# A graph network on one core: one-hot rows laid out two by two with 16-bit operands in the first stage, and gathered rows awaited by pairs of chunks in the first attention

## What is computed

```python
x = _layernorm(x + _L0_gnn_ref(x, src, dst, ...), axis=-1)   # attention, 8 heads
x = _layernorm(x + _L1_gnn_ref(x, ..., src, dst), axis=-1)   # attention, 4 heads
x = _layernorm(x + _L2_gnn_ref(x, src, dst, ...), axis=-1)   # 5 GIN layers
x = _layernorm(x + _L3_gnn_ref(x, edge_index, ...), axis=-1) # 3 SAGE layers
```

```python
Q = (text_emb @ Wq.T + bq).reshape(N, H, DK)
K = (text_emb @ Wk.T + bk).reshape(N, H, DK)
V = (x @ Wv.T + bv).reshape(N, H, DK)
Q_, K_, V_ = Q[col], K[row], V[row]
scores = jnp.sum(Q_ * (K_ + rel), axis=-1) / np.sqrt(DK)
e = jnp.exp(scores - segment_max(scores, col)[col])
attn = e / segment_sum(e, col)[col]
out = segment_sum(attn[:, :, None] * V_, col).reshape(N, OUT_DIM)
```

## Time and profile before

| | |
|---|---|
| median of 3 runs | 3004.7 us (3004.44 to 3008.03) |
| profiled execution | 3004.63 us, span 3002.9 us |
| mean granted clock of TensorE | 0.941 |
| busy share of the span | PE 88%, DVE 53%, ACT 38%, POOL 33% |
| `prepare` | from the start to about 146 us |
| attention of layer 0 | from about 148 us to about 696 us |

### The profile page before, as it was taken

The page is one execution under the profiler, slowest core; times in us unless marked ns, Lnnn a source line. Parts: engine busy times, 40 slices in busy tenths (PEclk is TensorE's granted clock), DMA queues, the critical chain, the costliest instruction groups (busy, mean ns, idle before and its releaser), DMA issues. The chain is left out here.

```text
span 3002.9 us, 53203 instructions
## 1 busy us (share of the span) xinstructions
PE 2653.7 (88%) x17164; PEld 1925.8 (64%) x17164; DVE 1592.7 (53%) x2777; ACT 1129.3 (38%) x3145; POOL 981.8 (33%) x1020
## 2 busy tenths in 40 slices
PE   6879999998537788877499999999999989999998
PEld 4769999996437777775265555655556556565654
DVE  9589999995568888886421512315123152121123
ACT  6135555554336777764310503105031052121111
POOL 4377777763367777773200100101001000000000
PEclk7889999999869999998599999999999999999999
DMA  6699999982337898884254252442524233444332
GB/s 229 228 312 319 316 317 317 316 295 85 104 85 148 152 162 148 152 161 74 87 182 134 63 152 75 135 131 60 152 74 135 74 109 95 115 119 134 114 112 92
DMA packets 332504, 470.20 MB, mean 157 GB/s; under 512 B 155942, under 2 KB 243062, under 8 KB 331588
## 3 DMA queue, kind: packets, MB, share of 16 engines
q1 hardware_dynamic: 269364, 286.33, 35.9%
q0 software_dynamic: 59088, 176.67, 19.0%
q10 hardware_dynamic: 3776, 3.80, 0.4%
HBM read 412.95 MB, written 55.50 MB: 156 GB/s over the span
## 5 line engine op out<-in xcount | busy, mean ns | idle before, releaser
L1144 ACT ACTIVATE sums<-e_part_ps 128x384 f32 x832 | 413.0, 496 | 382.8 <-PE e_part_ps L1042 291.7
L2464 PE MATMUL gin_sum_ps<-slab,high 128*128 128x391 f16 x2000 | 495.4, 331 | 2.0 <-DMA slab<-adj 1.6
L2464 PE MATMUL gin_sum_ps<-slab,low 128*128 128x391 f16 x1920 | 478.2, 331 | 0.0
L849 POOL DMA_INDIRECT e_from_src<-vk,src x416 | 393.3, 945 | 141.9 <-issue 95.4
L849 POOL DMA_INDIRECT e_from_src<-val,src x416 | 393.3, 946 | 134.0 <-issue 109.4
L2866 PE MATMUL sage_sum_ps<-slab,high 128*128 128x391 f16 x1200 | 389.5, 329 | 0.6 <-DVE x L3007 0.6
L2866 PE MATMUL sage_sum_ps<-slab,low 128*128 128x391 f16 x1152 | 379.3, 329 | 0.0
L2649 DVE SCALAR_TENSOR_TENSOR z_t<-h_t,gin_own,gin_sum_ps 128x391 f32<-128x391 f32 x80 | 44.8, 617 | 481.4 <-PE gin_sum_ps L2464 481.4
L1040 PE MATMUL e_part_ps<-e_onehot,e_from_src 128*128 128x129 f32 x1664 | 284.9, 296 | 13.8 <-ACT ends L1146 11.1
L2526 POOL TENSOR_SCALAR h_t<-h_t 128x391 f32<-128x391 f32 x32 | 40.1, 1263 | 770.5 <-DVE h_t L2679 770.5
L2464 PEld LDWEIGHTS gin_sum_ps<-slab,high 128*128 128x128 f16 x2000 | 195.2, 98 | 130.6 <-DVE low L2641 3.7
(11 more groups left out here) (402 smaller groups left out, 4354.1 us busy)
## 6 DMA issues: line engine op xcount, KB each, us to landing
slab<-adj SPq DMA_DIRECT2D x128, 977.5 KB, 4.8
e_window<-q_part SPq DMA_DIRECT2D x416, 128.0 KB
slab<-adj SPq DMA_DIRECT2D x32, 488.8 KB, 5.0
slab<-adj SPq DMA_DIRECT2D x32, 391.0 KB, 6.3
adj<-e_counts SPq DMA_DIRECT2D x8, 1250.0 KB
adj<-e_counts SPq DMA_DIRECT2D x8, 1193.8 KB
e_from_src<-vk,src POOLq DMA_INDIRECT x416
e_from_src<-val,src POOLq DMA_INDIRECT x416
```

The lines of the kernel that those rows point to most:

```text
L849: nc.gpsimd.indirect_dma_start(from_src[:, b, j, :], None, by_src, bass.IndirectOffsetOnAxis(ap=keep["src"][:, g * G + j:g * G + j + 1], a ...
L1144: nc.scalar.activation(keep["sums"][:, :, bass.ds(starts[j], P)], of[:, :, 0:P], ACT.Copy).then_inc(whole_copied, 1)
L2464: mm = nc.tensor.matmul(sum_ps[KH * n + m][:, 0:AN], part[:, t, m * P:(m + 1) * P], slab[:, s, n, k * AN:(k + 1) * AN], start=(t == 0 and ...
```

## The change

In `prepare` DVE makes all 16 one-hots of a round, ACT none. `is_row` gets the layout `[P, NB, 8, P, 2]`: two chunks lie side by side, row number by row number, so that the innermost pair of elements belongs to two chunks. The numbers 0 to 127 are written twice each (`row_numbers`, `[P, P, 2]`, float16, cast by POOL), and the operand `row_of` is now read as pairs of neighbouring elements, each pair 128 times. Every operand of the instruction is 16-bit with an innermost step of 1. PE reads its weights with a step of two elements. ACT's `spot_side`, its buffers, its two semaphores and the conversion `minus_row` (L378) go; `take_cells` and `take_turned` stand alone in ACT's program. In layer 0's attention each pair of chunks has its own semaphore (16 in place of 4), and each `match` waits for the two gathers of its pair.

```diff
-        iota16 = sb("iota16", [P, P], F16)
-        is_row = sb("is_row", [P, NB, STEP, P], F16)
+        row_numbers = sb("row_numbers", [P, P, 2], F16)
+        is_row = sb("is_row", [P, NB, STEP // 2, P, 2], F16)
...
-            nc.vector.tensor_scalar(minus_row[:, :], ints[:, 2, :], -1.0, None, ALU.mult).then_inc(row_set, 1)
...
-                nc.vector.tensor_tensor(is_row[:, u % NB, SIDE:STEP, :], iota16[:, :].unsqueeze(1).to_broadcast([P, STEP - SIDE, P]),
-                                        row_of[:, u * STEP + SIDE:(u + 1) * STEP].unsqueeze(2).to_broadcast([P, STEP - SIDE, P]),
-                                        ALU.is_equal).then_inc(rows_spotted, 1)
+                nc.vector.tensor_tensor(is_row[:, u % NB, :, :, :], row_numbers[:, :, :].unsqueeze(1).to_broadcast([P, STEP // 2, P, 2]),
+                                        row_of[:, u * STEP:(u + 1) * STEP].rearrange("p (q i) -> p q i", i=2).unsqueeze(2)
+                                        .to_broadcast([P, STEP // 2, P, 2]), ALU.is_equal).then_inc(rows_spotted, 1)
...
-            for u in range(STEPS):
-                spot_side(u)
-                if u in (9, 17, 25):
-                    take_cells(u // BANK - 1)
-                if u in (12, 20):
-                    take_turned(u // BANK - 1)
-            take_turned(2)
-            take_cells(3)
-            take_turned(3)
+            for q in range(4):
+                take_cells(q)
+                take_turned(q)
...
                 pe.wait_ge(rows_spotted, u + 1)
-                pe.wait_ge(side_spotted, u + 1)
...
-                    mm = nc.tensor.matmul(cell_ps[:, FOLD * c:FOLD * (c + 1)], is_row[:, u % NB, j, :],
+                    mm = nc.tensor.matmul(cell_ps[:, FOLD * c:FOLD * (c + 1)], is_row[:, u % NB, j // 2, :, j % 2],
...
-        src_in = sems(nc, ctx, *(f"e{layer}_src_in{b}" for b in range(RING)))
+        LANDED = 1 if layer else PAIRS
+        src_in = [sems(nc, ctx, *(f"e{layer}_src_in{b}_{i}" for i in range(LANDED))) for b in range(RING)]
...
-                        bass.IndirectOffsetOnAxis(ap=keep["src"][:, g * G + j:g * G + j + 1], axis=0)).then_inc(src_in[b], 16)
+                        bass.IndirectOffsetOnAxis(ap=keep["src"][:, g * G + j:g * G + j + 1], axis=0)).then_inc(src_in[b][j * LANDED // G], 16)
...
-                if pair == 0:
-                    v.wait_ge(src_in[b], 16 * G * it + 16 * G)
+                v.wait_ge(src_in[b][pair], 32 * (it + 1))
```

27 lines of the change are left out of this document (5 added, 22 removed).

## The result

The changed kernel takes 2988.12 us (median of 5 runs, 2982.74 to 2995.68). The kernel before, timed again beside it, took 3008.03 us (5 runs, 3004.44 to 3011.67). The ratio is 0.9933, with a 95% interval of 0.9921 to 0.9945, so about 20 us less. The forecast was 2990.7, in a range of 2986 to 2999: the number is 2.6 us off, but as a difference to the kernel before the forecast had 13.9 us and the ratio says 20.1 (16.5 to 23.8). The profiled execution took 2984.15 us, of it 2982.4 us span. The same kernel was measured twice more later on: 0.9949 (0.9929 to 0.9970) and 0.9934 (0.9920 to 0.9949).

A forecast was written before the change was run, and what follows sets the result against it. It took DVE to bound prepare's loop at full clock and PE at half, with PE, DVE and POOL within 1% in the first attention. Loop 10.4 plus attention 3.5, 13.9 us off 3004.6, gave 2990.7 us, range 2986 to 2999.

The forecast's parts named there:

- The spotting, 1.22 us: In prepare's loop, DVE's comparison making 2048 one-hot elements takes 1.22 us, at 0.52 ns an element plus a fixed part.
- The round at full clock, 1.58 us: In prepare's loop, waits through DVE and PE hold 3.15 us for two rounds, 1.58 each: 0.42 us saved a round.
- The round at half clock, nothing saved: In prepare's loop at half clock, PE is the bound and its 2.28 us a round stands, so nothing is saved.
- The loop, 10.4 us: Prepare's loop: 1.8 up to find_edges, 1.1 for two rounds, 7.8 for the last twelve, less 0.3, saves 10.4 us.
- Nothing changes behind the loop: Work from the loop's end to the attention moves earlier whole, with no gain of its own; 1 to 2 us allowed in range.
- The weight step, 0: PE reading placing weights at a step of two in prepare costs 0 to 30 ns a load, taken as 0.
- Rival B: Prepare's weight step costs 30 ns a load, 0.48 us a round, leaving 4.8 us gained: 2999.8 us; chance 0.06.
- ACT's work leaving, 0 by itself: Taking the one-hots from ACT in prepare's loop costs nothing and gives nothing by itself.
- The attention, 3.5 us: In the first attention, waits by pairs leave no wait for match's chunks, and ticks run at 9.94 us: 3.5 us saved.
- A: The faster rate does not come in prepare: spotting 2.28 us, round 2.53, total 3009.8 us, slower than before; chance 0.07.
- C: The clock stays half for long in prepare's loop, giving back 0.70 us a round: 2998.5 us; chance 0.04 wholly, 0.07 in part.
- D: Waits by pairs give nothing in the first attention, since transfers are as full as PE: 2994.2 us; chance 0.06.

The follow-up runs named there:

- e8: The full change with VectorE taking the Q tile of two rounds back instead of one: 2987.65 us, ratio 0.9912 to the kernel before.
- e2: The kernel before with only the attention's waits by pairs added: 3005.32 us, ratio 0.9981 to the kernel before.
- e12: The full change with VectorE taking Q from two rounds back and make_fold ahead of find_edges, no unread matmuls: 2987.50 us, ratio 0.9926.
- e5: The full change, but ScalarE still makes the first 4 of each 16 one-hots, in the new layout: 3001.14 us, ratio 0.9966.
- e4: The full change with the old one-hot layout, VectorE making all 16, waits by pairs kept: 3016.39 us, ratio 1.0026.
- e6: The full change plus 5 unread matmuls, two behind the seventh Q tile and three behind the ninth: 2992.94 us, ratio 0.9919.

## Why the prediction held, step by step

- *The spotting, 1.22 us:* right to the hundredth, 0.52 ns an element and 156 ns fixed against 0.52 and 155. The way to it was weaker than that. The row of 255 ns for 416 elements gives, less the 156 fixed, 0.24 ns an element and not the 0.26 that the prediction reads from it; twice 0.24 would have made 1.13 us. That two sources halve the rate was assumed, and no run tries it. What the runs show is half of the 1.04 ns that the old layout takes. The upper bound (2.28) is real: it is what the old layout takes for the same elements. The Trainium skill ("VectorE: DVE Perf Modes", "The perf-mode tier table") gives 1224 ns for such an operation, and the trace agrees with its 1215.
- *The round at full clock, 1.58 us:* 1.60 over twelve, and the two rows 1.71 and 1.47 show the loop of waits, since it holds two rounds. Taking it away (e8) gave the 1.47 that DVE alone was said to need.
- *The round at half clock, nothing saved:* right where PE is the bound (2.3 us from 31.65 to 33.97), but the four rounds from 9 to 13 took 8.78 us where they took 9.38. Of these 0.6 us 0.53 lie in the first one, right behind `make_fold`, where PE had caught up and DVE was the bound.
- *The loop, 10.4 us:* it was 12.7. Up to the start of `find_edges` 3.1 us against 1.8, and the prediction's most was 1.9: its wait for the gathers (0.49) went wholly, since POOL was done with them 4.9 us earlier (at 34.9 instead of 39.8), and the clock rose at 34 instead of 37 (0.7 us in round 4). From there to spotting 9 0.8 us against 1.1, rounds 9 to 13 0.6 against nothing, the last twelve rounds 7.6 against 7.8 less 0.3, and 0.5 for the last spotting, which the sum had forgotten. The last twelve met their number with some luck in the baseline: the same first stage took 1.7 us less for them in e2.
- *Nothing changes behind the loop:* this is the step that failed, by 3.2 us. The sum behind the loop took 4.9 us instead of 6.7, and from the node numbers to the attention's first instruction another 1.4 went. Before, PE was at half clock there (0.50 from 91 to 98), now at full clock. The fourteen executions bear it out: the sum took 4.9 to 5.1 us in the five that were at full clock throughout (and in e12, where the clock fell only 0.5 us before its end), and 6.3 to 8.3 in the other eight; from the node numbers to the first gather of the attention it was 52.0 to 52.5 us in those five and 53.0 to 54.0 in the other nine. The text had it as "1 to 2" in the lower end of the range only. The run with fillers behind the seventh and ninth Q tiles shows the term from the other side: with half clock from 78 to 83 the same sum took 7.3 us.
- *The weight step, 0:* 0.42 us for sixteen placings against 0.40. Rival B is out.
- *ACT's work leaving, 0 by itself:* right as put, though it is what lets the faster rate count (e5).
- *The attention, 3.5 us:* from its first DVE instruction to the merge 547.0 against 550.4 before, 3.4 us. Over all kernels the pairs are worth about 3. That no wait for a transfer would be left was nearly right (1.6 us), and what is late next is PE's spread, 34.4 us in 52 places against 29.7.
- *The rivals:* A was priced at 5.2 us over before and measured at 7.8 (e4); with the pairs of the change it did not come. C was right in kind, since the clock did move, but it went the other way. D is out by e2.
- *The signs:* spottings, both kinds of round and the placings read as forecast. The node numbers came at 80.6 (84.7 was forecast), the attention's first gather at 132.7 (138), its last `take_scores` at 659.4 (664.6), each 4 to 5 us ahead.

So the sum was 5.5 us short up to the attention, 2.3 in the loop and 3.2 behind it. Most of it, 3.9 us, has one reason: except in the last twelve rounds, the clock was carried over from the trace of before, and it stood higher in the changed kernel both in round 4 (0.7) and behind the loop (3.2). The rest is the wait for the gathers (0.5), the round behind `make_fold` (0.5) and the forgotten last spotting (0.5), with small terms of either sign. That the number 2990.7 lies nearer to 2988.12 than this is luck: the kernel before took 3008.03 us when it was timed again, and not 3004.7.

## What to carry to other kernels

Two operands that are broadcast can still be read as neighbours: lay the result out so that the innermost run is two elements long in every operand, and check that the reader's step doesn't cost. When one engine's part of a shared step becomes faster, work out the other's round before keeping the split: here ScalarE's 1.96 us took 5.1 of the loop's 12.7 us. Look also at engines that only run beside the step: here each gather on POOL took half the time. And work out a stage at either clock, since the same code met both. Last, judge a gain of a few us in an early phase by where the next phase starts, since one phase later on may scatter by more than the gain.

## What was not expected of the hardware

- The stretches at half clock lay at the same times within 1 us in three executions of the change, yet two kernels with the same first stage (before and e2) differ by a whole stretch (0.50 and 1.00 from 81 to 87), and e8 and e12, the same up to round 6, by 4.2 us in the first rise.
- The clock fell at 44.0 in the change, although TensorE's only idle stretch from 38.5 to 44 was 1.73 us long. With this gap and the next one filled (e6) it stayed at 1.00 through 44 to 54, and was then at 0.50 from 77.6 to 84.5, although it had been full for 40 us and the only idle stretch over 0.3 us just before was 0.95 us long, the same one that the change passed at full clock.
- POOL's gathers take 0.95 us each by the median behind the loop, where no spotting runs, but took 1.43 to 2.45 beside the old spottings of 1.75 us, 1.96 to 2.99 beside those of 2.28, and 0.94 to 1.92 beside the new ones (the five gathers ahead of `find_edges` in before, e4 and after).
- In the second attention DVE waited up to 11.4 us for one gather to land (e6; 4.1 in the change's first execution), beside stores of 1.2 MB to the adjacency, and the same code took from 512 to 528 us.
